# Folding pairs of score blocks with a relu ahead of the row maximum in the first self attention

## What is computed

```python
q = linear(x, qw).reshape(Bq, Nq, H, DH)          # k and v alike
sim = jnp.einsum('bihd,bjhd->bhij', q, k) * scale
attn = jax.nn.softmax(sim, axis=-1)
out = jnp.einsum('bhij,bjhd->bihd', attn, v).reshape(Bq, Nq, D)
return linear(out, ow, ob)
```

## Time and profile before

| What | Value |
|---|---|
| Median of three runs | 4216.11 us (4212.34 to 4227.01) |
| Profiled execution, first to last instruction | 4217.9 us |
| TensorE matmul, busy | 3909.5 us, 93% |
| VectorE, busy | 2770.9 us, 66% |
| ScalarE, busy | 1839.2 us, 44% |
| Mean granted clock of TensorE | 0.952 |

### The profile page before, as it was taken

How to read it: one execution, slowest core, us unless ns; L and a number is a source line. 1 busy time by engine, 2 the same in 40 slices (tenths; PEclk the granted TensorE clock), 3 DMA queues, 4 the chain that set the end, 5 groups by cost and what they waited for, 6 DMA issues and landing times. The chain is left out here.

```text
span 4217.9 us, 64445 instructions
## 1 busy us (share of the span) xinstructions
PE 3909.5 (93%) x24639; PEld 2598.3 (62%) x24639; DVE 2770.9 (66%) x4547; ACT 1839.2 (44%) x2746; POOL 1859.2 (44%) x1203
## 2 busy tenths in 40 slices
PE   3799999994998997998999999999999979999899
PEld 2533443433557886884666666666666647777787
DVE  6599999953536654435676767676766737665665
ACT  1267777771443333442333333333333334444333
POOL 1288970001203002005777777877787753222200
PEclk9789999996779998997999999999999989999899
DMA  4734434405622005883211111121112010000100
GB/s 159 180 56 77 59 57 48 42 2 94 102 43 52 22 13 197 306 308 103 75 51 51 64 63 51 51 76 51 51 51 76 26 31 10 10 10 1 42 15 17
DMA packets 314421, 294.96 MB, mean 70 GB/s; under 512 B 133420, under 2 KB 237292, under 8 KB 313860
## 3 DMA queue, kind: packets, MB, share of 16 engines
q1 hardware_dynamic: 311460, 281.88, 25.7%
q0 software_dynamic: 2656, 8.97, 0.7%
HBM read 161.92 MB, written 127.28 MB: 69 GB/s over the span
## 5 line engine op out<-in xcount | busy, mean ns | idle before, releaser
L1741 POOL TENSOR_TENSOR f_sums<-f_sums,f_probs 128x1024 f32<-128x1024 f32 x384 | 915.5, 2384 | 154.8 <-ACT f_probs L1860 117.1
L1860 ACT ACTIVATE f_probs<-f_st 128x1024 f32<-128x1024 f32 x512 | 525.0, 1027 | 938.7 <-PE f_st L1906 933.9
L1758 DVE TENSOR_REDUCE f_mx<-f_s 128x1 f32<-128x512 f32 x1024 | 659.8, 686 | 380.7 <-PE f_s L1883 369.4
L1369 DVE TENSOR_REDUCE f_mx<-f_s 128x1 f32<-128x512 f32 x1024 | 638.6, 683 | 50.8 <-PE f_s L1501 28.4
L1481 ACT ACTIVATE f_probs<-f_st 128x512 f32<-128x512 f32 x1024 | 535.9, 601 | 225.6 <-PE f_st L1518 225.5
L1883 PE MATMUL f_s<-f_k,f_q 64*128 64x512 f32 x3072 | 515.0, 415 | 18.6 <-DMA f_k<-k 12.5
L1906 PE MATMUL f_st<-f_q,f_k 64*128 64x512 f32 x3072 | 485.2, 390 | 1.1 <-ACT f_probs L1860 1.0
L1920 PE MATMUL f_acc<-f_probs,f_v 128*64 128x512 f32 x2048 | 465.0, 596 | 0.0
L1883 PEld LDWEIGHTS f_s<-f_k,f_q 64*128 64x128 f32 x3072 | 341.2, 189 | 166.6 <-issue 112.1
L1906 PEld LDWEIGHTS f_st<-f_q,f_k 64*128 64x128 f32 x3072 | 366.4, 184 | 25.9 <-ACT f_probs L1860 3.8
L1518 PE MATMUL f_st<-f_q,f_k 50*128 50x512 f32 x1024 | 332.7, 472 | 6.9 <-ACT f_probs L1481 6.8
(11 more groups left out here) (320 smaller groups left out, 7874.5 us busy)
## 6 DMA issues: line engine op xcount, KB each, us to landing
q<-f_stage SPq DMA_DIRECT2D x80, 512.0 KB, 2.9
k<-f_stage SPq DMA_DIRECT2D x80, 512.0 KB, 2.9
f_q<-q SPq DMA_DIRECT2D x32, 1024.0 KB, 5.0
f_k<-k SPq DMA_DIRECT2D x32, 1024.0 KB, 7.3
v<-f_v_stage SPq DMA_DIRECT2D x64, 256.0 KB, 3.1
f_v<-v SPq DMA_DIRECT2D x32, 512.0 KB, 8.5
f_q<-q SPq DMA_DIRECT2D x96, 128.0 KB, 4.2
f_k<-k SPq DMA_DIRECT2D x96, 128.0 KB, 6.9
```

The lines of the kernel that those rows point to most:

```text
L1369: v.tensor_reduce(mx[:, i % 2, c:c + 1], bank[u % 4][:, :], AX_X, ALU.max).then_inc(s_free, 1)
L1741: g_.tensor_tensor(out, out, probs[:, n % NP, :, :], ALU.add).then_inc(sum_done, 1)
L1758: v.tensor_reduce(mx[:, i % 2, c:c + 1], bank[u % 3][:, :], AX_X, ALU.max).then_inc(s_free, 1)
L1860: a_.activation(probs[:, s % NP, :, :], stb[s % 2][:, :, :], ACT.Exp, scale=L.scale).then_inc(p_ready, 1)
```

## The change

One head of four (j = 0, r = 1) in each second slot (`slot` even, j = 0) no longer has two score blocks a and b (key halves 0 and 1) in two banks with two maxima. One PSUM bank, `fold`, gets a − b: two matmuls accumulate, the second with a negated copy of the keys (`gap`). ScalarE replaces it in place by relu(a − b) (`rise`). A third matmul adds b (`lift`): relu(a − b) + b is the larger of the two, element by element. VectorE then takes one maximum over the 512 elements (`top_of_fold`). The bank is taken from the ring, which goes from four to three. `negative` makes the negated keys, once per step, on ScalarE. One column per head and query block of `mx` is no longer written and is set to −3e38 once by POOL.

TensorE issues `gap` ahead of the slot's scores and `lift` behind its values; ScalarE does `rise` between the slot's second and third exponential; VectorE takes the fold's maximum behind the slot's other maxima. The diff, cut to its core (every `u % 4` and `u - 3` becomes `u % 3` and `u - 2`, and the prologue is changed in the manner of the loop):

```diff
-        NP, DEPTH, EARLY, RING0 = 8, 3, 3, 4
+        NP, DEPTH, EARLY, RING0 = 8, 3, 3, 3
+        FOLDS = SLOTS // 2
+        def folded(slot):
+            return slot % 2 == 0
+        def fold_no(i, slot):
+            return i * FOLDS + slot // 2
...
-            bank = [ps(f"s{k}", [P, 512]) for k in range(4)]
+            bank = [ps(f"s{k}", [P, 512]) for k in range(3)]
+            fold = ps("fold", [P, 512])
+            k_neg = [sb(f"k_neg{k}", [P, HALF], F32R) for k in two]
...
+                g_.memset(mx[:, :, :], -3.0e38).then_inc(set_done, 1)
...
                 def top(i, slot, f):
-                    for r in range(2):
+                    for r in range(1 if folded(slot) else 2):
...
+                def top_of_fold(i, slot):
+                    dve.wait_ge(fold_ready, fold_no(i, slot) + 1)
+                    c = (2 * QB + slot // 2) * 2
+                    v.tensor_reduce(mx[:, i % 2, c:c + 1], fold[:, :], AX_X, ALU.max).then_inc(fold_free, 1)
                 def negate(i):
+                    dve.wait_ge(fold_free, (i + 1) * FOLDS)
...
+                        if n < STEPS and folded(slot):
+                            top_of_fold(n, slot)
                         if s == SLOTS - EARLY - 1 and i + 1 < STEPS:
                             negate(i + 1)
...
+                def negative(i):
+                    act.wait_ge(q_in[i % DEPTH], (i // DEPTH + 1) * QLOADS)
+                    if i >= 2:
+                        act.wait_ge(gap_ready, (i - 1) * FOLDS)
+                    a_.activation(k_neg[i % 2][64:64 + SROWS, :], k_[i % DEPTH][64:64 + SROWS, 0, HALF:N], ACT.Copy,
+                                  scale=-1.0).then_inc(negated, 1)
+                def rise(i, slot):
+                    act.wait_ge(gap_ready, fold_no(i, slot) + 1)
+                    a_.activation(fold[:, :], fold[:, :], ACT.Relu).then_inc(gap_cut, 1)
...
+                        if s == 10 and i + 2 < STEPS:
+                            negative(i + 2)
                         for e in range(4):
+                            if e == 2 and n_ < STEPS and folded(slot):
+                                rise(n_, slot)
...
+                def gap(i, slot):
+                    cur, rows, qs = i % DEPTH, slice(64, 64 + SROWS), slice(slot // 2 * P, slot // 2 * P + P)
+                    if slot == 0:
+                        pe.wait_ge(negated, i + 1)
+                    if fold_no(i, slot) > 0:
+                        pe.wait_ge(fold_free, fold_no(i, slot))
+                    t.matmul(fold[:, :], q[cur][rows, 0, qs], k_[cur][rows, 0, 0:HALF], start=True, stop=False, tile_position=(64, 0))
+                    t.matmul(fold[:, :], q[cur][rows, 0, qs], k_neg[i % 2][rows, :], start=False, stop=True,
+                             tile_position=(64, 0)).then_inc(gap_ready, 1)
+                def lift(i, slot):
+                    pe.wait_ge(gap_cut, fold_no(i, slot) + 1)
+                    t.matmul(fold[:, :], q[cur][rows, 0, qs], k_[cur][rows, 0, HALF:N], start=False, stop=True,
+                             tile_position=(64, 0), skip_group_check=True).then_inc(fold_ready, 1)
                 def score(i, slot, f):
+                    if folded(slot) and f == 0:
+                        gap(i, slot)
-                    for r in range(2):
+                    for r in range(1 if folded(slot) else 2):
-                        pe.wait_ge(s_free, u - 3)
+                        pe.wait_ge(s_free, u - 2)
...
                         if s < LAG and i > 0:
                             values(i - 1, SLOTS + s - LAG)
+                        if n < STEPS and folded(slot):
+                            lift(n, slot)
```

More of the change, by code:

```diff
@@ L1252, in attend_narrow @@
                     if n < STEPS:
-                        unit("s", n, slot, f, 0), unit("s", n, slot, f, 1)
+                        for r in range(1 if folded(slot) else 2):
+                            unit("s", n, slot, f, r)
                     if f == 0 and s == SLOTS - EARLY and i + 1 < STEPS:
@@ L1291, in attend_narrow @@
             s_ready, s_free = sem("s_ready"), sem("s_free")
+            negated, gap_ready, gap_cut, fold_ready, fold_free = (sem(s) for s in (
+                "negated", "gap_ready", "gap_cut", "fold_ready", "fold_free"))
             negm_done, m_cut = sem("negm"), sem("m_cut")
@@ L1377, in turned @@
                     u, par = at["turn", i], i % 2
-                    rows = bank[u % 4][0:4 * QB, 0:P]
+                    rows = bank[u % 3][0:4 * QB, 0:P]
                     dve.wait_ge(s_ready, u + 1)
@@ L1388, in normalise @@
                     half, g, u = n % 2, n // 2 % 2, at["back", n // 2, n % 2]
-                    view = bank[u % 4][:, :].rearrange("p (b h w) -> p b h w", b=4, w=W)
+                    view = bank[u % 3][:, :].rearrange("p (b h w) -> p b h w", b=4, w=W)
                     dve.wait_ge(s_ready, u + 1)
@@ L1420, in _ @@
                         top(0, slot, f)
+                    if folded(slot):
+                        top_of_fold(0, slot)
                 negate(0)
@@ L1425, in _ @@
                         top(1, slot, f)
+                    if folded(slot):
+                        top_of_fold(1, slot)
                 for i in range(STEPS + 1):
@@ L1463, in high @@
                         act.wait_ge(s_ready, at["y", (n // 2 // NG) * NG - 1, half, 1] + 1)
-                    a_.activation(o_hi[:, ch, half * HALF:(half + 1) * HALF], bank[u % 4][:, :], ACT.Copy).then_inc(hi_done, 1)
+                    a_.activation(o_hi[:, ch, half * HALF:(half + 1) * HALF], bank[u % 3][:, :], ACT.Copy).then_inc(hi_done, 1)
+                def negative(i):
[7 more added lines that the diff above has]
+                    a_.activation(fold[:, :], fold[:, :], ACT.Relu).then_inc(gap_cut, 1)
+                act.wait_ge(set_done, 6)
+                negative(0)
+                for slot in range(0, SLOTS, 2):
+                    rise(0, slot)
+                    if slot == 0:
+                        negative(1)
+                for slot in range(0, EARLY, 2):
+                    rise(1, slot)
                 for i in range(STEPS + 1):
@@ L1496, in score @@
                         pe.wait_ge(q_in[cur], (i // DEPTH + 1) * QLOADS)
-                    for r in range(2):
+                    if folded(slot) and f == 0:
+                        gap(i, slot)
+                    for r in range(1 if folded(slot) else 2):
                         u = at["s", i, slot, f, r]
                         rows = slice(64 * r, 64 * r + SROWS)
-                        pe.wait_ge(s_free, u - 3)
-                        t.matmul(bank[u % 4][:, :], q[cur][rows, j, qb * P:(qb + 1) * P], k_[cur][rows, j, f * HALF:(f + 1) * HALF],
+                        pe.wait_ge(s_free, u - 2)
+                        t.matmul(bank[u % 3][:, :], q[cur][rows, j, qb * P:(qb + 1) * P], k_[cur][rows, j, f * HALF:(f + 1) * HALF],
                                  start=True, stop=True, tile_position=(64 * r, 0)).then_inc(s_ready, 1)
@@ L1506, in turn @@
                     pe.wait_ge(negm_done, i + 1)
-                    pe.wait_ge(s_free, u - 3)
-                    t.transpose(bank[u % 4][0:4 * QB, 0:P], negm[:, :], ident[:, :]).then_inc(s_ready, 1)
+                    pe.wait_ge(s_free, u - 2)
+                    t.transpose(bank[u % 3][0:4 * QB, 0:P], negm[:, :], ident[:, :]).then_inc(s_ready, 1)
                 def shifted(i, s, j):
@@ L1536, in back @@
                     pe.wait_ge(o_ready, n + 1)
-                    pe.wait_ge(s_free, u - 3)
+                    pe.wait_ge(s_free, u - 2)
                     for k in range(4):
-                        ins = t.transpose(bank[u % 4][:, k * P:(k + 1) * P], osb[:, half, k * P:(k + 1) * P], ident[:, :])
+                        ins = t.transpose(bank[u % 3][:, k * P:(k + 1) * P], osb[:, half, k * P:(k + 1) * P], ident[:, :])
                     ins.then_inc(s_ready, 1)
@@ L1544, in rows @@
                     pe.wait_ge(s_free, at["back", n // 2, half] + 1)
-                    pe.wait_ge(s_free, u - 3)
+                    pe.wait_ge(s_free, u - 2)
                     for k in range(4):
-                        ins = t.transpose(bank[u % 4][:, k * P:(k + 1) * P], on[:, half, k, :], ident[:, :])
+                        ins = t.transpose(bank[u % 3][:, k * P:(k + 1) * P], on[:, half, k, :], ident[:, :])
                     ins.then_inc(s_ready, 1)
@@ L1559, in project @@
                                                            for o, w in ((o_hi, w_hi), (o_hi, w_lo), (o_lo, w_hi))):
-                                ins = t.matmul(bank[u % 4][:, k * D:(k + 1) * D], o[:, ch, tok], w[:, ch, :],
+                                ins = t.matmul(bank[u % 3][:, k * D:(k + 1) * D], o[:, ch, tok], w[:, ch, :],
                                                start=n == 0, stop=n == 3 * DC - 1)
@@ L1566, in _ @@
                         score(0, slot, f)
+                    if folded(slot):
```

(3 more changed lines are left out.)

12 lines of the change are left out of this document (8 added, 4 removed).

## The result

The changed kernel takes **4331.43 us** (median of 4 runs, 4327.33 to 4340.08), the kernel before 4214.85 in the same measurement: a ratio of 1.0271 [1.0247, 1.0294], so it is slower by 117 us. The forecast was 4320, with a range of 4280 to 4350. The profiled execution took 4330.63 us with a span of 4328.6, 110.7 more than before.

The account below looks back on a forecast made before the run. A loop of TensorE and ScalarE, not VectorE's maxima, was taken to set the pace. Terms 111 (wait at a3) − 5 (turn) − 2 (prologue) = +104 us on 4216 gave 4320 us, range 4280 to 4350.

Parts of the forecast that it names:

- What bounds the kernel: First self attention: a loop of TensorE and ScalarE over three `st` banks sets the 2.61 us slot; maxima only fit.
- The wait at a3: Fourth score of the plain slot waits for the bank of that slot's first score: +0.93 us per pair, 111 us.
- B: Folded slot, 118 in the steps with scores; its loop was to keep 2.61 us, bounds 0 and +0.2 each.
- the 0.54: Time in us from lift's start, behind the values, to the fold's maximum; 0.43 was the lower end.
- the 0.11: Cost in us of a tiling-mode change, paid by lift: the term is 111 us; paid elsewhere, 98.
- B stretches too: Rival: same-row matmuls or a long relu delay the fourth shifted matmul or lift; up to 24 us more, 4344; chance 0.14.
- Turn backs: Plain slots that turn outputs back, with five units: +0.97 us in place of +0.93, so counted with the rest.
- The turn: In a folded slot of 3.21 us: the wait for negated maxima goes, 15 × 0.32 = −5 us (bounds 0 and −9).
- The projections: Three plain slots whose projection matmuls cover the wait; left in the sum, at most 3 us too much.
- A slots: Plain slots after folded ones, 119 in the steps with scores; forecast to last about 3.5 us.
- The prologue: Maxima before the loop: 4.4 to 4.5 us per pair against 4.78, plus 0.65 for the first copy: −2 us.
- It waits for the step's loads ... no wait: Negated-key copy on ScalarE, in the slot behind the eviction: loads issued by 424.75, slot starts at 436.85, costing nothing.

## Why the prediction was right

**What bounds the kernel** held. The reading of a slot with scores against one without was confirmed by the run with one more reduce per slot: 49 us of extra work on VectorE, no time.

**The wait at a3** held to a hundredth. The prediction had, after lift, the fold's maximum at 0.54, a3's load at 1.88, the values at 2.54, B at 3.54 and the next lift at 6.15; measured were 0.54, 1.88, 2.55, 3.54 and 6.15. Between the 0.54 and the 0.43 it chose the 0.54 behind values, and that is what came. The Trainium skill, TensorEngine Tiling (Array Packing), section Tiling Modes (Key Properties), has a change of tiling mode drain TensorE; by that rule the prediction let lift pay the 0.11 and the shifted matmul behind it nothing. The trace has the 0.54 at lift, but it doesn't single lift out: the shifted matmul that starts beside it (440.25) has its exponential 0.57 later, and the score at 442.13, with no values ahead of it, lasts 0.50 us as lift does, where the scores at 444.13 last 0.39. In these three the weight load starts together with its matmul; at 444.13 it ran 0.23 ahead. So why it is 0.54 at lift stays open. The run with the moved score showed the cause of the wait at a3 and not only its length.

**B** kept 2.61, with 0.42 us of TensorE's load waiting for the first exponential (0.30 before): the rival "B stretches too" did not come. There was more in hand than the 0.05 us foretold, as B's matmuls had been laid out too long: the score of the other row half starts with the gap matmul (both at 444.13), not behind it, and the third shifted matmul starts 0.81 into B (444.60), not 1.03. The relu has a mean of 603 ns (0.60 taken), starts 1.51 into B at 445.30 (1.52 foretold) and ends 0.50 before lift.

**Turn backs** were given +0.97: 3.18 became 4.13, +0.95. **The turn** was given −0.32 in its B slot: from 3.2 and 3.4 us in turn it fell to about 2.8 in 14 steps, −0.54 on average; the prediction had read a slot of 3.2 alone. **The projections** were left in as A slots at +0.93, called at most 3 us too much: the three A slots grew by 0.22 each (5.39 to 5.61), the B slots before them by 0.24. With these the 15 steps were to grow by 111 − 5 − at most 3, 103 to 106 us; it was 102.6.

**The prologue** was the mis-sized term: −2 us forecast (bounds −4 and +4), +8 measured. The pair itself was right: lifts at 229.72 and 234.21 are 4.49 apart for 4.4 to 4.5. The failed step is "It waits for the step's loads ... no wait", which was checked for the copies in the loop alone. The second copy stands in the prologue, ahead of the second relu, and its keys come 12.35 us later. The prediction had 0.65 for the first copy, and for the second neither a price nor what queues behind it. With the copy moved, the run above took 44.4 us from its first score to its first shifted matmul, where the kernel before took 45.7 and after 53.3.

**The tail** was in no term. Near the end of the stage of after, in its profiled execution, four slots take 4.07 us and their neighbours 3.70 and 3.26, as ScalarE waits for shifted matmuls at half the clock. The table by stretches of after, and a group of exponentials from its timeline:

```profile
1025.00:1030.00 5.00, 4.16 (x24) 1.27 (x24) 0.00 (x0) 3.92 (x9) 0.00 (x0) 1.00 0.00 0
...
1035.00:1040.00 5.00, 4.74 (x17) 1.19 (x20) 0.00 (x0) 3.01 (x7) 0.00 (x0) 0.50 0.00 0
...
1055.00:1060.00 5.00, 4.85 (x32) 1.86 (x28) 0.69 (x1) 4.42 (x10) 0.00 (x0) 1.00 0.00 0
```

```profile
1038.01 2.08 ACT L1532 ACTIVATE f_probs<-f_st 128x512 f32<-128x512 f32 x4 [1.99 <-PE f_st L1587]
```

It is not in the profile of before, nor in those of the later fold's maximum and of the later copy. But shorter falls of the same kind lie in the last step of three other profiles, two of them without a fold: with one more reduce (the granted clock is 0.67 from 910 to 915 us, and two slots take 3.69 and 4.42), with the moved score (3.61 and 4.42), some 4 us each, and briefly with TensorE's order spread. So the fold isn't needed for it. Whether every run of after has it stays open, as does what brought it on: the slots there are the same as before.

Against a sum of +104, the two profiles are 110.7 apart: about −3 in the 15 steps, +10 in the prologue, +7 in the tail and −7 behind the stage. That the last two cancel is luck. The medians, 4331.43 and 4214.85, are 117 apart; where the other 6 us lie the two profiles don't show.

## What to carry to other kernels

A high busy share is no bound: compare a slot with the work to a slot without it, in the same trace, before work is taken from an engine. When a change takes a bank from a ring, find which instruction needs the bank of which, and count from the event that frees it: here one bank fewer, freed one queue place later, cost 0.93 us per pair, and 64 us of maxima saved gave nothing. Work on data that comes later does not go into an in-order queue ahead of work that is due now, and each copy of a moved step, the first one too, needs its own look at what queues behind it.

## What the runs showed beyond what was expected

**The clock stayed low in a stage that is busy.** The table by stretches of the kernel before, where it rises:

```profile
234.00:239.00 5.00, 5.00 (x27) 1.29 (x25) 3.69 (x7) 3.09 (x6) 4.79 (x3) 0.77 1.61 91
239.00:244.00 5.00, 5.00 (x36) 2.02 (x32) 4.75 (x9) 3.91 (x9) 4.74 (x4) 1.00 0.25 22
```

TensorE is busy all 5 us there, and the clock goes from 1.2 to 2.4 GHz. With three banks it was busy 64.62 of 70 us and stayed at 1.2 GHz until about 399 us, which cost about 58 us. In the tail of after it fell to 1.2 GHz with TensorE busy 4.16 of 5 us shortly before, and came back some 20 us later; the kernel before, busy 42.52 of 50 us in its last stretch, kept 1.00 there. What made the difference no run here shows. None of this was in the prediction or in the expectation of the run with three banks.

**A relu from PSUM into PSUM in place** costs what an exponential from PSUM does: 603 ns against 598 at 128x512.
